# Long attention on one core: the shift products, the weighted sums and the banks for maxima rearranged

## Chip, cores and metric

One core of a Trainium2 chip runs the whole program. The metric is the device time of one execution in microseconds (us), the median of several executions; lower is better.

## What is computed

Four layers of cross-attention, each with a feed-forward part behind it, on 16 batches of 56 tokens. Layers 1 to 3 attend with 16 heads over 1500 keys of 64 numbers, and these three attentions are the "long attention" that the change touches. Cut to what matters, for one batch:

```
scores = jnp.einsum('bhsr,bhlr->bhsl', q_r, k_r)     # 16 heads x 56 tokens, 1500 keys
attn   = jax.nn.softmax(scores, axis=-1)
ctx_c  = jnp.einsum('bhsl,bld->bhsd', attn, kv_rope)
out    = ctx_lat.reshape(b, s, H * K) @ Wo.T
```

The softmax needs the maximum over the keys for each of the 16 x 56 = 896 rows (the shift, which is subtracted before the exponential) and the sum of the exponentials.

## The kernel before

`attend_long` runs one layer's long attention. Its queries stand as 64 numbers on partitions and 896 columns, cut in two halves e = 0 and 1 of 448 columns; the keys and queries are held twice, on partitions 0 to 63 and 64 to 127, so that products with 64 rows for e = 0 and e = 1 run side by side on the two row halves of TensorE's array. The 1500 keys are cut in 12 units of 125. A batch has three rounds of four units; there are 16 batches in a layer and three layers, so 48 batches and 144 rounds. In each layer batches 0 to 3 and 12 to 15 are written out, batches 4 to 11 run in a loop (`Fori`).

**Scores.** For a unit, `score` issues four steps (part 0 to 3) of two products each, e = 0 and 1: keys high x query high, keys low x query high, keys high x query low, and the shift. The last multiplies a tile of ones (`on`, 64 rows) with `sh`, whose row 64e holds the negated maxima and whose other rows are zero. All four add up in one PSUM bank for each e: unit u uses banks 2(u mod 2) and 2(u mod 2) + 1. The first part waits until ScalarE has taken the unit before the last out of them (`exp_done`), the last signals `st_ready`.

**Exponentials.** ScalarE's `exps` reads both banks of a unit (125 x 896) and writes one of four ring buffers `ex`.

**Weighted sums.** After the 16 steps of a round, PE issues `weigh` for the four units of that round in one burst: plain float32 products, values (125 rows x 64 columns) against `ex`, e = 0 to the lower and e = 1 to the upper 64 output columns. They go to bank 4.

**Maxima.** The next batches' maxima are computed ahead: 21 pieces in a batch (seven tiles of 128 query rows, three stretches of 500 keys), each one product with 64 rows (`top_scores`, alternating between the row halves) and one reduction on VectorE (`tops`), through banks 6 and 7; a piece waits until the piece before the last is reduced. `PLACES` says before which step of a round (0 to 16) each of its seven pieces goes. When all 21 are done VectorE reduces them to `nm` (128 x 7), PE turns `nm` through bank 5 with a float32 product (`turn`, after the burst of the second round), ScalarE copies the result (`high`), and SP moves it to `sh` with four DMAs (`shifts`).

**Row sums.** GpSimd and VectorE add the exponentials of a round up (`gather`, `pair`); after the first round of the next batch PE sums over partitions (`sums_by_quarters`, 32 output columns, bank 5) and ScalarE copies that out (`row_sums`). `numerators` copies bank 4 after the last burst of the batch, in ScalarE's order after the batch's exponentials.

**SP** runs one list for each batch b, behind a wait for all weighted sums of batch b - 1: loads of keys and queries for b + 2, of their low parts for b + 1, then the row sums, the shifts for b + 1, and the scales.

The lines are: 1174 score products, 1181 maxima products, 1196 turn, 1206 weighted sums, 1214 sums by quarters, 1271 and 1276 reductions of maxima, 1283 `pair`, 1341 exponentials, 1347 `numerators`, 1359 `high`, 1109 shift DMAs. Elsewhere in the program, and untouched: line 433 (products with 64 rows and 96 columns of weights), line 2145 (128 rows and 128 columns), line 133 (products that keep PE running).

Of the kernel before, what the change touches and what calls it, by code (L numbers as in the profile page):

```python
# [13 lines left out]
FP32 = mybir.dt.float32  # L14
# [998 lines left out]
def attend_long(nc, G, l, ctxT):  # L1013
# [10 lines left out]
    with Stage(nc, f"att{l}") as st:  # L1024
        kh, q, top, nm, nmh = (G[n] for n in ("kh", "qt", "top", "nm", "nmh"))
# [19 lines left out]
        WEIGHED, SUMMED = 4, 5  # L1045
# [16 lines left out]
        PLACES = (0, 0, 6, 8, 10, 14, 16)  # L1062
# [16 lines left out]
        with nc.Block() as block:  # L1079

            @block.sync
            def _(sp):
# [20 lines left out]
                def shifts(b):  # L1103
                    s = b % 2
                    sp.wait_ge(high_done, b + 1)
                    for e, at, tiles, a, z in ((0, 0, (0, 3), 0, 128), (0, 384, (3, 4), 0, 64),
                                               (1, 0, (3, 4), 64, 128), (1, 64, (4, NT), 0, 128)):
                        n = (tiles[1] - tiles[0]) * (z - a)
                        sp.dma_start(sh[64 * e:64 * e + 1, s, at:at + n].rearrange("o (t p) -> o t p", p=z - a).bitcast(FP32),
                                     nmh[tiles[0]:tiles[1], s, a:z].bitcast(FP32)).then_inc(m_in[s], 16)  # L1110
# [26 lines left out]
                sp.wait_ge(ones, 1)  # L1137
# [18 lines left out]
            def _(pe):  # L1156
                def products(s, u, e):

                    rows, keys = slice(64 * e, 64 * e + 64), slice(KP * u, KP * u + KP)
                    high = q[rows, s, HALF * e:HALF * e + HALF]  # L1160
                    return ((kh[rows, s, keys], high), (kl[rows, s % 2, keys], high),
                            (kh[rows, s, keys], ql[rows, s % 2, :]), (on[rows, :], sh[rows, s % 2, :]))

                def score(s, b, u, part, first):

                    if part == 0 and not (known(b, 1) and u < 2):
                        pe.wait_ge(exp_done, UNITS * b + u - 1)
                    if u == 0 and part == 1:
                        pe.wait_ge(kl_in[s % 2], of_two(s, b, 64))
                    if u == 0 and part == 3:  # L1170
                        pe.wait_ge(m_in[s % 2], of_two(s, b, 64))
                    for e in (first, 1 - first):
                        k, rhs = products(s, u, e)[part]
                        last = pe.matmul(PS[2 * (u % 2) + e][0:KP, 0:HALF], k, rhs, start=part == 0, stop=part == 3)  # L1174
                    if part == 3:
                        last.then_inc(st_ready, 1)

# [6 lines left out]
                def top_scores(s, b, n, half):  # L1184
# [3 lines left out]
                    if not (known(b, 1) and n < 2):  # L1188
                        pe.wait_ge(mx_done, PIECES * b + n - 1)
                    maxima(6 + (PIECES * s + n) % 2, s, n, half).then_inc(mx_ready, 1)  # L1190

                def turn(s, b):
                    pe.wait_ge(nm_ready, b + 1)
                    if not known(b, 2):
                        pe.wait_ge(sm_done, b - 1)
                    pe.matmul(PS[SUMMED][0:NT, 0:128], nm[:, s % 2, :], G["ident"][:, :],
# [12 lines left out]

                def sums_by_quarters(total):  # L1210
# [7 lines left out]
                def sums(totals):  # L1218

                    for n, total in enumerate(totals):  # L1220
                        for e in range(2):
                            last = pe.matmul(PS[SUMMED][64 * e:64 * e + 64, 0:HALF], one[:, :], total[:, e, :],
# [36 lines left out]
                pe.wait_ge(ones, 3)  # L1259
                emit(pe, batch)  # L1260
                pe.wait_ge(sm_done, B - 1)
# [6 lines left out]
            def _(dve):  # L1268
                def tops(s, b, n):
                    dve.wait_ge(mx_ready, PIECES * b + n + 1)  # L1270
                    dve.tensor_reduce(top[:, s % 2, n // NS, n % NS:n % NS + 1], PS[6 + (PIECES * s + n) % 2][:, 0:SB],  # L1271
                                      AX.X, ALU.max).then_inc(mx_done, 1)

                def shift(s, b):
                    dve.wait_ge(mx_done, PIECES * b + PIECES)
                    dve.tensor_reduce(nm[:, s % 2, :], top[:, s % 2], AX.X, ALU.max, negate=True).then_inc(nm_ready, 1)
# [20 lines left out]
                def batch(s, b, left):  # L1297
                    for i in range(UNITS // 4):
                        for place in range(17):
# [10 lines left out]
                for t in range(NT):  # L1310
# [3 lines left out]
                    dve.tensor_reduce(nm[:, 0, t:t + 1], scored, AX.XY, ALU.max, negate=True).then_inc(mx_done, NS)  # L1314
                dve.wait_ge(mx_done, PIECES)
                dve.engine_nop().then_inc(nm_ready, 1)
# [5 lines left out]
                dve.reciprocal(rsb[:, 1, :], PS[SUMMED][:, 0:HALF]).then_inc(last_inverted, 1)  # L1322
# [6 lines left out]
            def _(act):  # L1329
# [25 lines left out]
                def high(s, b):  # L1355
# [3 lines left out]
                    act.activation(nmh[:, s % 2, :], PS[SUMMED][0:NT, 0:128],  # L1359
                                   ACT.Copy).then_inc(high_done, 1)  # L1360

                def batch(s, b, left):
                    for i in range(UNITS // 4):
                        for u in range(4 * i, 4 * i + 4):
# [3 lines left out]
                        if i == 1 and left:  # L1368
                            high((s + 1) % 4, b + 1)
                    if left:  # L1370
                        numerators(s, b)
# [5 lines left out]
            def _(pool):  # L1377
                pool.wait_ge(G["q_out"][1], HALF_STORES * l)
# [25 lines left out]
                pool.wait_ge(ones, 3)  # L1404
# [1101 lines left out]
```

## Time and profile before

| | |
|---|---|
| median of 3 executions | 2348.38 us (2343.8 to 2348.43) |
| the profiled execution's own time | 2348.98 us |
| its span, first to last instruction | 2347.2 us |
| PE busy | 2203.3 us (94%) |
| PE weight loads busy | 1538.0 us (66%) |
| VectorE busy | 1476.7 us (63%) |
| GpSimd busy | 1093.4 us (47%) |
| ScalarE busy | 950.1 us (40%) |

Each stage of the program has its own limit, so the shares of the whole span say little about one of them; the stage is read by windows and by the timeline of one batch. PE's times in the trace are the start of a product and a modelled end: products that follow each other overlap there, so distances between starts tell the pace. A burst that the timeline merges ends with its last product, whose own duration has to be taken off to get that product's start.

### The profile page before, as it was taken

The page shows a single profiled execution, that of the slowest core. Times are in us where ns is not written, and L with a number is a line of the kernel's source. Part 1 is how long each engine was busy: PE and PEld are TensorE (multiplying, and loading weights), DVE is VectorE, ACT ScalarE, POOL GpSimd, SP SyncE. Part 2 cuts the span into 40 slices and gives each one's busy share as a digit, 9 for nine tenths or more (in the row PEclk, how much of TensorE's full clock was granted, in tenths as well). Part 3 has the DMA queues.
Part 4 walks back from the last instruction along what each step waited for, and adds up shares of the span by engine and source line. Part 5 has one row for each costly group of instructions (what it writes and reads, how often), then busy time and mean ns, then how long its engine had stood idle before and what let it go on. Part 6 is the DMA issues. An engine that isn't in the chain of part 4 may idle for free. (4 is left out here: it accounts for less than half of the span.)

```text
span 2347.2 us, 38608 instructions
## 1 busy us (share of the span) xinstructions
PE 2203.3 (94%) x13814; PEld 1538.0 (66%) x13814; DVE 1476.7 (63%) x2468; ACT 950.1 (40%) x1433; POOL 1093.4 (47%) x612
## 2 busy tenths in 40 slices
PE   6768999999999998999999999898999999998998
PEld 4447998665555557666555555897655555577997
DVE  2775444577777757787777775412777777744444
ACT  2442443434455442113544454112354455424443
POOL 0330332047777760563777777101177777722332
PEclk9878999999999999999999999898999999998999
DMA  4472732474555513226455451384845446303332
GB/s 83 131 249 84 224 116 81 114 174 99 136 116 116 121 30 126 60 81 149 99 124 128 103 135 30 123 336 181 237 94 129 110 108 136 74 5 111 116 116 82
DMA packets 124358, 285.60 MB, mean 122 GB/s; under 512 B 33371, under 2 KB 76207, under 8 KB 120476
## 3 DMA queue, kind: packets, MB, share of 16 engines
q1 hardware_dynamic: 123548, 281.96, 44.8%
q8 instruction: 82, 1.34, 0.3%
q0 software_dynamic: 672, 1.84, 0.2%
q14 instruction: 56, 0.46, 0.1%
HBM read 237.15 MB, written 46.41 MB: 121 GB/s over the span
## 5 line engine op out<-in xcount | busy, mean ns | idle before, releaser
L1271 DVE TENSOR_REDUCE keep_top<-banks 128x1 f32<-128x500 f32 x945 | 604.2, 675 | 241.9 <-PE banks L1181 236.3
L1341 ACT ACTIVATE att_ex<-banks 125x896 f32<-125x896 f32 x576 | 524.3, 919 | 236.3 <-PE banks L1174 216.8
L1206 PE MATMUL banks<-att_ex,att_v 125*64 125x448 f32 x2304 | 464.7, 545 | 0.0
L1394 POOL TENSOR_TENSOR att_acc<-att_acc,att_ex 125x896 f32<-125x896 f32 x186 | 391.8, 2106 | 74.0 <-ACT att_ex L1341 60.8
L1394 POOL TENSOR_TENSOR att_acc<-att_acc,att_two 125x896 f32<-125x896 f32 x141 | 297.2, 2108 | 161.4 <-DVE att_two L1283 161.4
L1181 PE MATMUL banks<-keep_kh,keep_qt 64*128 64x500 f32 x1230 | 369.8, 420 | 2.6 <-PEq L598 1.2
L1206 PEld LDWEIGHTS banks<-att_ex,att_v 125*64 125x64 f32 x2304 | 152.5, 136 | 247.1 <-issue 188.4
L1174 PE MATMUL banks<-att_sh,att_on 64*125 64x448 f32 x1152 | 296.7, 365 | 0.0
L1174 PE MATMUL banks<-att_ql,keep_kh 64*125 64x448 f32 x1152 | 296.1, 363 | 0.0
L1709 PE MATMUL banks<-moe_xs,moe_w 128*128 128x448 f32 x1272 | 285.6, 374 | 5.4 <-DVE moe_w L1805 3.8
L1283 DVE TENSOR_TENSOR att_two<-att_ex 125x896 f32<-125x896 f32 x144 | 243.1, 1688 | 59.6 <-ACT att_ex L1341 57.2
L1709 PEld LDWEIGHTS banks<-moe_xs,moe_w 128*128 128x128 f32 x1272 | 243.2, 192 | 31.1 <-DVE moe_w L1805 4.6
L1795 POOL TENSOR_TENSOR moe_sc<-moe_sg,moe_cb 128x448 f32<-128x448 f32 x106 | 122.5, 1156 | 292.5 <-ACT moe_sg L1767 263.1
L1174 PE MATMUL banks<-keep_qt,keep_kh 64*125 64x448 f32 x1152 | 246.7, 403 | 8.0 <-ACT att_ex L1341 2.7
L1181 PEld LDWEIGHTS banks<-keep_kh,keep_qt 64*128 64x128 f32 x1230 | 178.7, 187 | 86.7 <-issue 59.5
L1174 PE MATMUL banks<-keep_qt,att_kl 64*125 64x448 f32 x1152 | 217.4, 363 | 0.0
L1818 DVE TENSOR_TENSOR moe_hf<-banks,moe_sc 128x448 f32<-128x448 f32 x106 | 66.2, 625 | 201.4 <-POOL moe_sc L1795 201.4
L1174 PEld LDWEIGHTS banks<-att_sh,att_on 64*125 64x125 f32 x1152 | 177.3, 183 | 15.3 <-DMA att_sh<-keep_nmh 0.3
L1174 PEld LDWEIGHTS banks<-att_ql,keep_kh 64*125 64x125 f32 x1152 | 173.6, 183 | 6.4
L1174 PEld LDWEIGHTS banks<-keep_qt,keep_kh 64*125 64x125 f32 x1152 | 108.9, 182 | 74.5 <-ACT att_ex L1341 53.4
L1394 POOL TENSOR_TENSOR att_acc<-att_ex 125x896 f32<-125x896 f32 x48 | 101.1, 2107 | 103.2 <-ACT att_ex L1341 103.2
L789 POOL TENSOR_TENSOR q_tc<-q_tc,q_ts 96x896 f32<-96x896 f32 x32 | 67.6, 2111 | 113.0 <-DVE q_ts L777 113.0
(271 smaller groups left out, 2725.5 us busy)
## 6 DMA issues: line engine op xcount, KB each, us to landing
keep_kh<-kvt_hi SPq DMA_DIRECT2D x96, 375.0 KB, 5.2
att_kl<-kvt_lo SPq DMA_DIRECT2D x96, 375.0 KB, 7.3
q_rows<-mats_q SPq DMA_DIRECT2D x24, 896.0 KB, 4.9
keep_qt<-q_rows SPq DMA_DIRECT2D x96, 224.0 KB, 5.9
moe_raw<-L_experts_dram SPq DMA_DIRECT2D x53, 384.0 KB, 4.2
att_v<-kvn SPq DMA_DIRECT2D x24, 720.0 KB
sort_wu<-L_experts_dram SPq DMA_DIRECT2D x14, 1024.0 KB, 8.3
moe_cb<-comb_rows SPq DMA_DIRECT2D x62, 224.0 KB
```

The lines of the kernel that those rows point to most:

```text
L789: pool.tensor_tensor(tc[:, u % 4], tc[:, u % 4], ts[:, u % 2], ALU.add).then_inc(rot_done, 1)
L1174: last = pe.matmul(PS[2 * (u % 2) + e][0:KP, 0:HALF], k, rhs, start=part == 0, stop=part == 3)
L1181: return pe.matmul(PS[bank][:, 0:SB], q[rows, s, 128 * t:128 * t + 128], kh[rows, s, SB * c:SB * c + SB], start=True, stop=True)
L1206: last = pe.matmul(PS[WEIGHED][64 * e:64 * e + 64, 0:HALF], v[:, s // 2, u, s % 2, :], ex[:, u % RING, e, :], start=u == 0, stop=u == UNIT ...
L1271: dve.tensor_reduce(top[:, s % 2, n // NS, n % NS:n % NS + 1], PS[6 + (PIECES * s + n) % 2][:, 0:SB], AX.X, ALU.max).then_inc(mx_done, 1)
L1283: dve.tensor_tensor(two[:, i], ex[:, 2], ex[:, 3], ALU.add).then_inc(paired, 1)
L1341: act.activation(ex[:, u % RING], scored, ACT.Exp).then_inc(exp_done, 1)
L1394: pool.tensor_tensor(a, a if n else ex[:, 0], two[:, i] if k == 2 else ex[:, k], ALU.add).then_inc(gathered, 1)
L1709: last = pe.matmul(PS[2 * e + m][:, 0:HALF], w[:, s, pw, o:o + 128], xs[:, px, k, HALF * e:HALF * e + HALF], start=n == 0, stop=n == 3 * K ...
L1795: pool.tensor_tensor(sc[:, e, :], sg[:, e, :], cb[:, s, HALF * e:HALF * e + HALF], ALU.mult).then_inc(comb_done, 1)
L1818: dve.tensor_tensor(hf[:, e, :], PS[2 * e + 1][:, 0:HALF], sc[:, e, :], ALU.mult).then_inc(h_made, 1)
```

## The change

- **Shifts.** Steps 0 to 2 of a unit stay. The fourth, for one unit, goes; instead `shift_two` issues one step of four products for two units u (even) and u + 1, each on a strip of 32 rows (rows 0, 32, 64, 96 of `sh` and `on` start the strips), into the four banks of the two units. It closes unit u and opens unit u + 1, and stands between them. `free`, the wait for the bank, moves with it. A pair of units has seven steps instead of eight.
- **Weighted sums.** `weigh_two` issues the sums of two units, after step 6 (those of the two units before) and at the end of a round (those of its first two units). A round has two bursts of two units, lagging by two; the last two units of a batch are weighed in the first round of the next, and after the last batch on their own. `numerators` moves behind the second exponential of the next batch, and SP's list of a batch waits for that later burst.
- **Maxima.** Three banks 5, 6, 7 in turn; a piece waits for the piece three before. The row sums use bank 6 and the turn bank 7 in between, with waits for what was there (`mx_done`, `sm_done`, `high_done`). `PLACES` is new, for 15 places.
- **Turn.** `nm` becomes 64 x 128 (in the fast float32 format, zeroed at the start by GpSimd), written by two reductions of 64 partitions each; it is turned by one product with 64 rows and 64 columns against a small identity, at the start of the third round. `nmh` is 14 x 64, and the four DMAs each bring seven rows of 64 numbers. The first batch's maxima go the same way.

```diff
-        PLACES = (0, 0, 6, 8, 10, 14, 16)
+        PLACES = (1, 4, 6, 7, 9, 11, 13)
+        SHARED = 2 * NT + 2
...
+                    for row in range(0, 128, 32):
+                        a = NT * (row // 64)
+                        sp.dma_start(sh[row:row + 1, s, :].rearrange("o (g j) -> o g j", j=64).bitcast(FP32),
+                                     nmh[a:a + NT, s, :].bitcast(FP32)).then_inc(m_in[s], 16)
...
-                            (kh[rows, s, keys], ql[rows, s % 2, :]), (on[rows, :], sh[rows, s % 2, :]))
+                            (kh[rows, s, keys], ql[rows, s % 2, :]))
+
+                def free(b, u):
+                    if not (known(b, 1) and u < 2):
+                        pe.wait_ge(exp_done, UNITS * b + u - 1)
...
+                def shift_two(s, b, u):
+
+                    free(b, u + 1)
+                    if u == 0:
+                        pe.wait_ge(m_in[s % 2], of_two(s, b, 64))
+                    for odd in range(2):
+                        for e in range(2):
+                            rows = slice(64 * e + 32 * odd, 64 * e + 32 * odd + 32)
+                            last = pe.matmul(PS[2 * odd + e][0:KP, 0:HALF], on[rows, :], sh[rows, s % 2, :],
+                                             start=odd == 1, stop=odd == 0)
+                        if odd == 0:
+                            last.then_inc(st_ready, 1)
...
-                    maxima(6 + (PIECES * s + n) % 2, s, n, half).then_inc(mx_ready, 1)
+                    pe.wait_ge(mx_done, PIECES * b + n - 2)
+                    if n == SHARED and not known(b, 2):
+                        pe.wait_ge(sm_done, b - 1)
+                    if n == TURNED - MAXIMA:
+                        pe.wait_ge(high_done, b)
+                    maxima(MAXIMA + n % 3, s, n, half).then_inc(mx_ready, 1)
...
-                    pe.matmul(PS[SUMMED][0:NT, 0:128], nm[:, s % 2, :], G["ident"][:, :],
+                    pe.wait_ge(nm_ready, 2 * b + 2)
+                    pe.matmul(PS[TURNED][:, 0:64], nm[:, s % 2, :], eye[:, :],
...
+                def weigh_two(s, b, u):
+
+                    for v in (u - 2, u - 1):
+                        if v >= 0:
+                            weigh(s, b, v)
+                        elif not known(b, 1):
+                            weigh((s - 1) % 4, b - 1, UNITS + v)
...
                 def batch(s, b, left):
                     for i in range(UNITS // 4):
                         half = 0
-                        for place in range(17):
+                        if i == 2 and left:
+                            turn((s + 1) % 4, b + 1)
+                        for place in range(15):
                             for ahead, n in pieces(i, place, left):
                                 top_scores((s + ahead) % 4, b + ahead, n, half)
                                 half = 1 - half
-                            if place < 16:
-                                score(s, b, 4 * i + place // 4, place % 4, half)
-                        for u in range(4 * i, 4 * i + 4):
-                            weigh(s, b, u)
+                            u, step = 4 * i + place // 7 * 2, place % 7
+                            if place < 14:
+                                if step == 3:
+                                    shift_two(s, b, u)
+                                else:
+                                    score(s, b, u + step // 4, step % 4, half)
+                            if place == 6:
+                                weigh_two(s, b, u)
+                        weigh_two(s, b, 4 * i + 2)
                         if i == 0 and not known(b, 1):
                             pe.wait_ge(gathered, GATHERS * b)
-                            pe.wait_ge(high_done, b + 1)
+                            if left:
+                                pe.wait_ge(mx_done, PIECES * b + PIECES + SHARED - 2)
                             sums_by_quarters(acc[:, (s + 1) % 2])
-                        if i == 1 and left:
-                            turn((s + 1) % 4, b + 1)
...
+                    for side in range(2):
+                        dve.tensor_reduce(nm[:, s % 2, side:2 * NT:2], top[64 * side:64 * side + 64, s % 2],
+                                          AX.X, ALU.max, negate=True).then_inc(nm_ready, 1)
...
                         for u in range(4 * i, 4 * i + 4):
                             exps(b, u)
+                            if u == 1 and not known(b, 1):
+                                numerators((s - 1) % 4, b - 1)
```

## Rows read from the trace of the kernel before

**Rows 1.** The page: span, busy time of engines, tenths by slice, PE's clock.
```profile
span 2347.2 us, 38608 instructions
PE 2203.3 (94%) x13814; PEld 1538.0 (66%) x13814; DVE 1476.7 (63%) x2468; ACT 950.1 (40%) x1433; POOL 1093.4 (47%) x612
...
PE   6768999999999998999999999898999999998998
...
PEclk9878999999999999999999999898999999998999
```
**Rows 2.** Windows: length, busy (x) PE, PEld, DVE, ACT, POOL, clock, DMA share, GB/s.
```profile
1092.43:1116.54 24.11, 24.11 (x178) 13.99 (x176) 18.50 (x26) 12.21 (x15) 16.83 (x8) 1.00 0.42 94
1286.95:1311.39 24.44, 24.23 (x177) 14.30 (x175) 18.98 (x27) 12.08 (x16) 17.98 (x9) 1.00 0.52 118
```
**Rows 3.** Timeline, PE, one loop batch: start, length, engine, line, shapes, count.
```profile
1286.95 3.23 PE L1206 MATMUL banks<-att_ex,att_v 125*64 125x448 f32 x16
1290.11 0.39 PE L1196 MATMUL banks<-ident,keep_nm 128*7 128x128 f32 x2
1290.42 0.49 PE L1181 MATMUL banks<-keep_kh,keep_qt 64*128 64x500 f32 x2
1290.76 0.36 PE L1174 MATMUL banks<-keep_qt,keep_kh 64*125 64x448 f32 x2
...
1291.56 0.37 PE L1174 MATMUL banks<-keep_qt,keep_kh 64*125 64x448 f32 x2
...
1292.43 0.36 PE L1174 MATMUL banks<-att_sh,att_on 64*125 64x448 f32 x1
1292.82 0.47 PE L1174 MATMUL banks<-keep_qt,keep_kh 64*125 64x448 f32 x2
...
1294.79 0.39 PE L1181 MATMUL banks<-keep_kh,keep_qt 64*128 64x500 f32 x1
...
1295.11 3.23 PE L1206 MATMUL banks<-att_ex,att_v 125*64 125x448 f32 x16
1298.27 0.50 PE L1181 MATMUL banks<-keep_kh,keep_qt 64*128 64x500 f32 x2
...
1303.04 0.60 PE L1206 MATMUL banks<-att_ex,att_v 125*64 125x448 f32 x2
```
**Rows 4.** Timeline, PE, behind the first round's burst of that batch.
```profile
1306.19 0.58 PE L1214 MATMUL banks<-att_acc,att_one 125*32 125x224 f32 x8
1306.71 0.49 PE L1181 MATMUL banks<-keep_kh,keep_qt 64*128 64x500 f32 x2
1307.04 0.37 PE L1174 MATMUL banks<-keep_qt,keep_kh 64*125 64x448 f32 x2
```
**Rows 5.** Line 1206 from 1286.9 to 1290: ns min/median/max, first and last start.
```profile
L1206 PE MATMUL banks<-att_ex,att_v x16: 539/539/590, 1287.0 to 1289.6; 125*64 125x448 f32 x16
```
**Rows 6.** Line 1174, whole span, the same columns; who waited for it.
```profile
L1174 PE MATMUL banks<-keep_qt,keep_kh x1152: 356/365/733, 490.5 to 2071.2; 64*125 64x448 f32 x192
...
  ACT att_ex L1341: 216.8, 290
```
**Rows 7.** Another stage, timeline, PE: 64-row products, then 128-row ones.
```profile
915.49 0.36 PE L433 MATMUL banks<-weights_wkr,weights_wqr 64*96 64x64 f32 x1
915.78 1.33 PE L2145 MATMUL banks<-weights_wc,weights_wq 128*128 128x192 f32 x3
```
**Rows 8.** That place by windows, and line 2145 there.
```profile
914.60:916.80 2.20, 2.20 (x19) 2.08 (x18) 2.17 (x2) 0.91 (x2) 0.00 (x0) 0.50 0.00 0
...
L2145 PE MATMUL banks<-weights_wc,weights_wq x5: 527/528/687, 915.8 to 917.2; 128*128 128x192 f32 x5
```
**Rows 9.** Timeline, VectorE, end of a second round.
```profile
1286.59 1.26 DVE L1271 TENSOR_REDUCE keep_top<-banks 128x1 f32<-128x500 f32 x2 [0.31 <-PE banks L1181]
1287.89 0.17 DVE L1276 TENSOR_REDUCE keep_nm<-keep_top 128x7 f32<-128x21 f32 x1
1288.08 1.91 DVE L1283 TENSOR_TENSOR att_two<-att_ex 125x896 f32<-125x896 f32 x1
```
**Rows 10.** Timeline, ScalarE: copy of the sums, then two exponentials.
```profile
1273.95 0.55 ACT L1347 ACTIVATE att_cu<-banks 128x448 f32<-128x448 f32 x1 [2.39 <-PE banks L1206]
1275.34 1.94 ACT L1341 ACTIVATE att_ex<-banks 125x896 f32<-125x896 f32 x2 [0.84 <-PE banks L1174]
```
**Rows 11.** Timeline, SP's queue: shift DMAs, then the next batch's loads.
```profile
1266.22 2.72 SPq L1109 DMA_DIRECT2D att_sh<-keep_nmh  x4
...
1274.17 1.24 SPq L626 DMA_DIRECT2D keep_kh<-kvt_hi  x2
```

More of the change, by code:

```diff
@@ L1024, in attend_long @@
     with Stage(nc, f"att{l}") as st:
-        kh, q, top, nm, nmh = (G[n] for n in ("kh", "qt", "top", "nm", "nmh"))
+        kh, q, top, nm, nmh, eye = (G[n] for n in ("kh", "qt", "top", "nm", "nmh", "eye"))
         kl = st.sb("kl", [128, 2, L], F32R)
@@ L1136, in _ @@
                 load_values(0)
-                sp.wait_ge(ones, 1)
+                sp.wait_ge(ones, 3)
                 shifts(0)
@@ L1221, in sums @@
                         for e in range(2):
-                            last = pe.matmul(PS[SUMMED][64 * e:64 * e + 64, 0:HALF], one[:, :], total[:, e, :],
+                            last = pe.matmul(PS[LAST_SUMMED][64 * e:64 * e + 64, 0:HALF], one[:, :], total[:, e, :],
                                              start=n == 0, stop=n == len(totals) - 1)
@@ L1258, in _ @@
                         maxima(half, 1, n, half)
-                pe.wait_ge(ones, 3)
+                pe.wait_ge(ones, 5)
                 emit(pe, batch)
+                for u in range(UNITS - 2, UNITS):
+                    weigh(3, B - 1, u)
                 pe.wait_ge(sm_done, B - 1)
@@ L1298, in batch @@
                     for i in range(UNITS // 4):
-                        for place in range(17):
+                        for place in range(15):
                             for ahead, n in pieces(i, place, left):
@@ L1313, in _ @@
                     scored = PS.all[:, a:a + NS * 512].rearrange("p (c k) -> p c k", c=NS)[:, :, 0:SB]
-                    dve.tensor_reduce(nm[:, 0, t:t + 1], scored, AX.XY, ALU.max, negate=True).then_inc(mx_done, NS)
+                    dve.tensor_reduce(top[:, 0, t, 0:1], scored, AX.XY, ALU.max).then_inc(mx_done, NS)
                 dve.wait_ge(mx_done, PIECES)
-                dve.engine_nop().then_inc(nm_ready, 1)
+                dve.wait_ge(ones, 2)
+                for side in range(2):
+                    dve.tensor_reduce(nm[:, 0, side:2 * NT:2], top[64 * side:64 * side + 64, 0, :, 0:1],
+                                      AX.X, ALU.max, negate=True).then_inc(nm_ready, 1)
                 for n in range(NT):
@@ L1363, in batch @@
                     for i in range(UNITS // 4):
+                        if i == 2 and left:
+                            high((s + 1) % 4, b + 1)
                         for u in range(4 * i, 4 * i + 4):
                             exps(b, u)
+                            if u == 1 and not known(b, 1):
+                                numerators((s - 1) % 4, b - 1)
                         if i == 0 and not known(b, 1):
                             row_sums(b - 1)
[L1368 to L1371, printed above, removed]
                 high(0, 0)
@@ L1377, in _ @@
             def _(pool):
+                pool.memset(nm[:, :, :].bitcast(FP32), 0.0).then_inc(ones, 1)
+                pool.tensor_copy(eye[:, :], G["ident"][0:64, 0:64]).then_inc(ones, 1)
                 pool.wait_ge(G["q_out"][1], HALF_STORES * l)
@@ L1402, in place @@
                     pool.tensor_tensor(ctxT[:, :, b * S:b * S + S], c, r, ALU.mult).then_inc(placed, 1)
-                pool.wait_ge(ones, 3)
+                pool.wait_ge(ones, 5)
                 for b in range(B):
```

37 lines of the change are left out of this document (14 added, 23 removed).

## The prediction

> **What bounds the kernel now.** I read the page first: PE is busy for 94% of the span, at nearly full clock [rows 1]. Long attention is half of the program: 48 batches of some 24.3 us. The windows are cut from burst to burst of weighted sums, three rounds each. A batch that is written out takes 24.11 us with PE busy for all of it, one in the loop 24.44 us with 24.23 us busy, both at clock 1.00, while VectorE has 18.5 to 19.0 us of work, GpSimd 16.8 to 18.0 us and ScalarE 12.1 to 12.2 us [rows 2]. So PE sets the pace. Half the batches are loop batches, so I take 24.27 us as the mean. Busy does not mean streaming at full pace, so next comes the timeline of PE [rows 3, 4], read by distances between starts.
>
> A step of two products takes 0.20 us (four steps from 1290.76 to 1291.56, 0.203 each, which I use). Weighted sums: 16 instructions in two columns, eight distances between the burst's start at 1286.95 and the end of its work; the last one starts at 1286.95 + 3.23 - 0.54 = 1289.64 [rows 3, 5], so seven distances take 2.69 us: 0.375 each, and 0.05 more for the first, which is 0.590 long instead of 0.539 [rows 5]. Eight are 3.00 us.
>
> **What a change of shape costs.** The array is used in pieces of different shapes: 64 rows and all columns (scores, maxima), all rows and 64 columns (weighted sums), all rows and 32 columns (sums by quarters). From the last start of a burst to what follows is 1290.11 - 1289.64 = 0.47 us instead of 0.375: 0.095 late. The first product of the new shape then waits openly for its weights: the score products after the turn and the maxima come at +0.33 (1290.42 to 1290.76), where the 500 columns of a maxima product are worth 500/448 of 0.187, 0.21: 0.12 more. Into a burst it is 1295.11 - 1294.79 = 0.32 against 0.21 (0.10 late) and the 0.05 above. In and out of a burst together: 0.10 + 0.05 + 0.095 + 0.12 = 0.37 us; with 125 instead of 128 columns of weights I take 0.35.
>
> **A round without waiting.** 16 steps (3.25), the opening pair of maxima (0.33), five more pieces, three of them on the busier row half (3 x 0.21 = 0.62), into the burst (0.10): 4.30 us. Measured from the first maxima to the next burst: 1290.42 to 1295.11 = 4.69 and 1298.27 to 1303.04 = 4.77 [rows 3], and 1306.71 to 1311.39, the window's end, 4.68 [rows 2, 4]. So 0.41 us of a loop round is waiting. It lies where unit 2 opens: 1292.43 to 1292.82 is 0.39 instead of 0.20, and that product lasts 0.47 instead of 0.36, its weights come openly too. ScalarE's exponential of unit 0 is what it waits for: bank and exponential run in lockstep. A written-out batch is 0.33 us shorter, 0.1 a round, so on average 0.36 us a round is waiting.
> The whole round before is 4.30 + 3.16 (burst, 1295.11 to 1298.27) + 0.36 = 7.82 us, with 0.32 a batch for the turn (1290.11 to 1290.42) and 0.52 for the sums by quarters (1306.19 to 1306.71) [rows 3, 4]. Check: 3 x 7.82 + 0.84 = 24.3.
>
> **The change, part by part.**
> 1. *Waits for exponentials.* In the new order every wait has a burst in front of it. The exponential of an odd unit can begin at step 6 and is wanted at the next `shift_two`, behind a burst of 1.85 us and three steps; it needs 0.36 for the product to land and 0.92 (1.94 for two [rows 10] with a gap). That of an even unit is wanted at the next pair, behind three steps and a burst. Gain: 0.36 x 144 rounds = -52 us. ScalarE's `numerators` sits behind a burst that ends some 2.1 us after step 6, takes 0.55 [rows 10], and is over at 2.7, before the next shift's product at about 3.2: no cost; if that cover went, 0.5 us a batch.
> 2. *Two shift steps fewer a round.* Four became two: -2 x 0.203 = -0.41 us a round, -58 us, if four strips run side by side. No row shows four row strips. The nearest shows four column strips: eight products of 224 columns start within 0.52 - 0.095 us, that is, four in 0.2 [rows 4]. I take full overlap; the other end is two by two, +0.2 us a shift.
> 3. *Two bursts instead of one.* The products stay; one more in and out a round: +0.35 us, +50 us. It takes about what part 1 gives.
> 4. *The strips' own change of shape.* Scores use 64 rows, shifts 32, so each of the 288 shifts goes in and out. No row shows 64 against 32. The nearest change of rows alone is elsewhere: the last product of line 433 (64 rows) starts at 915.49, the first of line 2145 (128 rows, all columns as before) at 915.78, 0.29 later [rows 7]. This is at clock 0.50, 1.2 GHz [rows 8]. A float32 product of 64 columns costs 0.375 x 64/448 x 2 = 0.107 there. So it is 0.18 late, 0.09 at 2.4 GHz, the same 0.095 as above, and the first product is 0.687 long instead of 0.528 [rows 8], 0.16, or 0.08 at full clock, of open weight load. Rows alone thus cost what columns cost. One way: 0.095 + 0.08 to 0.12. Both ways: 0.35 to 0.43, I take 0.38. Ends: 0 (rows of 64 and 32 go together) and 0.43. 288 x 0.38 = +109 us.
> 5. *Turn.* One fast product of 64 columns in the shape of the scores replaces two slow ones with a shape of their own; 0.32 falls to about 0.1: -0.22 x 48 = -10 us. It now follows a burst of two units. VectorE ended the maxima at 1287.85 and their reduction at 1288.06, 1.1 us after that burst's start [rows 9]. With two reductions (0.17 each) and a piece issued one step before the burst, I expect 1.2 to 1.5 us, and the turn is due at 1.65. No cost, with little to spare.
> 6. *Three banks.* Before, pieces waited in no visible place; they still don't. The new wait of the sums by quarters is for a piece issued before that burst of 1.65 us, done in 1.1 to 1.4. No cost. Behind both waits stands all of PE's queue, so being late would be paid in full.
> 7. *SP.* Its list for a batch starts 3.7 us later. Loads went out at 1274.17 [rows 11] and the first of them are wanted at the third round, some 16 us later: nothing. The shift DMAs take 2.72 to issue [rows 11] and are wanted one round later; four again. GpSimd's zeroing and VectorE's extra reduction at a layer's start: +0.4 us a layer, +1.
>
> The sum a round: 12 steps 2.44; four stretches with one piece on the busier half, 4 x 0.21 = 0.83; two bursts of 1.50 + 0.35, 3.70; two shifts of 0.20 + 0.38, 1.16: 8.13 us against 7.82, +0.31. In the parts it is -0.36 - 0.41 + 0.35 + 0.76 = +0.34. I take +0.33 x 144 = 48, -10 for the turn, +1: **+39 us**. The profiled execution took 2348.98 us, 1.8 us more than its span and 0.6 above the median. Forecast 2348.98 + 39 = **2388 us**, with part 4's price between 0.30 and 0.43 and 10 us for the small terms between 2365 and 2412.
>
> The Trainium skill, in "TensorEngine Tiling (Array Packing)", section Tiling Modes, Key Properties, says "Changing tiling mode (not just tile) drains the TensorE", and lists 64-row and 32-row tiling as two modes. The 0.29 us of [rows 7] agree for 64 against 128 rows; no row shows 64 against 32. By this rule the change loses, as the forecast does. The skill's "TensorE: Matmul & The Clock Gate", Part 3, gives 3.07 times for four row strips instead of four. As an estimate from that page a shift would take 1.30 steps, and the sum would be 288 x 0.06 = 17 us more; [rows 4] speak for full overlap of column strips only.
>
> **The rivals.**
> - *Strips of 32 rows mix freely with 64* (part 4 costs nothing). For it: both cut the array in rows only, and weights of one row half load under products of the other all the time. Against it: [rows 7]. Time: 2388 - 109 = 2279 us (2262 to 2300). This is the one on the other side: the sum turns at a price of 0.38 - 39/288 = 0.245 us a shift; below that the change is faster.
> - *The array drains, but the weights are loaded by then* (0.19 a shift): 2388 - 0.19 x 288 = 2333 us.
> - *New waits take the place of the old.* Turn and sums by quarters come late because VectorE's `pair` (1.91 here beside GpSimd [rows 9]) gets ahead of the last pieces: 0.3 us each, 0.6 x 48 = 29: 2417 us.
> - *Four strips run two by two*: 288 x 0.2 = 58: 2446 us.
>
> **How the numbers follow.** Forecast 0.69, free mixing 0.16, drain alone 0.08, new waits 0.04, two by two 0.03. 0.2%, or 4.7 us, is about what a measurement of this kernel can tell from no change. Faster: 0.16 + 0.08 = 0.24. Same: 0.04, taken from the forecast's chance for a price near 0.245 us a shift. Slower: 0.65 + 0.04 + 0.03 = 0.72. The forecast's own range is 2365 to 2412. Since the other sign has a quarter, the range goes down into free mixing and up to the new waits: 2285 to 2422.
>
> **What would show it.** Shift products with 32 rows some 0.29 us after the step before, and the step after them 0.38 later with a first product of 0.46: part 4 right; distances of 0.20: free mixing. No ScalarE wait before line 1174 (216.8 us of ScalarE's own waiting for scores [rows 6] would grow): part 1. Bursts of eight instructions and 1.85 us from in to out: part 3. Batches of about 25.1 us: the sum. The forecast is wrong above all if the small change of rows is cheaper than the large one.

## The result and the profile after

The changed kernel takes **2403.52 us** in the median (2401.56 to 2410.25), against 2346.09 us for the kernel before (2339.82 to 2348.43): 1.0255 times as long over all executions, 95% interval 1.0234 to 1.0276 (the two medians alone give 1.0245). The forecast was 2388 us, slower, in a range up to 2422; so the direction and the range hold, and the loss is 57 us by the medians where 39 were forecast. The forecast added its 39 us to 2348.98 us, an execution 3 us above the median, so the time itself is off by less than the loss.

The page of the changed kernel, its span, engine shares, clock and some of the costliest groups (columns as in [rows 1] and in the section of groups):

```profile
span 2400.9 us, 38704 instructions
PE 2254.9 (94%) x13766; PEld 1462.9 (61%) x13766; DVE 1403.5 (58%) x2519; ACT 948.7 (40%) x1433; POOL 1090.9 (45%) x618
...
PEclk9878999999999998999999999888999999998999
...
L1383 ACT ACTIVATE att_ex<-banks 125x896 f32<-125x896 f32 x576 | 525.6, 919 | 503.8 <-PE banks L1190 479.9
...
L1190 PE MATMUL banks<-att_sh,att_on 32*125 32x448 f32 x1152 | 136.4, 464 | 1.8 <-DMA att_sh<-keep_nmh 1.8
```

PE executes 48 instructions fewer and is busy 52 us longer: the same share of a longer span, so the loss is in PE's own pace, not in idle time. ScalarE now waits 479.9 us for scores where it waited 216.8 [rows 6], but most of that rise is waiting that stood in front of its other copies before: its idle time as a whole went from 1397.1 to 1452.2 us (span less busy time), no more than the span grew. What shows that PE no longer waits for it is PE's timeline. A window over one loop batch, then PE's timeline of half a round (columns as in [rows 2] and [rows 3]; lines 1177 are the score products, 1198 the maxima, 1190 the shifts, 1224 the weighted sums, 1214 the turn):

```profile
619.88:645.26 25.38, 25.38 (x176) 12.59 (x174) 17.20 (x28) 12.10 (x16) 17.90 (x9) 1.00 0.44 101
```
```profile
632.57 0.36 PE L1177 MATMUL banks<-att_ql,keep_kh 64*125 64x448 f32 x2
632.86 1.72 PE L1224 MATMUL banks<-att_ex,att_v 125*64 125x448 f32 x8
634.52 0.50 PE L1198 MATMUL banks<-keep_kh,keep_qt 64*128 64x500 f32 x1
634.52 0.46 PE L1177 MATMUL banks<-keep_qt,keep_kh 64*125 64x448 f32 x1
...
634.86 0.36 PE L1177 MATMUL banks<-keep_qt,keep_kh 64*125 64x448 f32 x1
...
635.25 0.38 PE L1177 MATMUL banks<-att_ql,keep_kh 64*125 64x448 f32 x2
635.56 0.47 PE L1190 MATMUL banks<-att_sh,att_on 32*125 32x448 f32 x4
635.96 0.48 PE L1198 MATMUL banks<-keep_kh,keep_qt 64*128 64x500 f32 x1
635.96 0.47 PE L1177 MATMUL banks<-keep_qt,keep_kh 64*125 64x448 f32 x1
636.27 0.36 PE L1177 MATMUL banks<-keep_qt,att_kl 64*125 64x448 f32 x1
...
636.69 0.37 PE L1177 MATMUL banks<-att_ql,keep_kh 64*125 64x448 f32 x2
636.99 0.60 PE L1224 MATMUL banks<-att_ex,att_v 125*64 125x448 f32 x2
```

All is there to be read. The four shift products run together (four in 0.47 us, the length of one). They start 0.31 us after the start of the last score step (635.25 to 635.56), where a step is 0.20; what follows comes 0.40 later, and the step after that another 0.31 instead of 0.20, with a first product of 0.47 instead of 0.36. The burst of two units stands between 632.86 and 634.52, 1.66 us for 1.50 of products, with the same open wait for weights behind it. No distance is left that would be a wait for ScalarE, as 0.39 us at unit 2 was [rows 3]. A half round is 4.13 us (632.86 to 636.99), and six of them with 0.1 for the turn and 0.5 for the sums by quarters are the 25.38 us of the batch, against 24.11 and 24.44 [rows 2].

There is one more loss, of another kind, in the same trace. At the end of the first pass of the third layer's loop PE stands idle twice with no semaphore to wait for, and runs at a lower clock behind it:

```profile
1924.91 1.72 PE L1224 MATMUL banks<-att_ex,att_v 125*64 125x448 f32 x8
...
1928.32 0.47 PE L1177 MATMUL banks<-keep_qt,keep_kh 64*125 64x448 f32 x2 [1.68 <-issue]
1931.11 0.78 PE L1198 MATMUL banks<-keep_kh,keep_qt 64*128 64x500 f32 x1 [2.33 <-issue]
```
```profile
1924.91:1935.07 10.16, 6.16 (x29) 3.11 (x27) 3.58 (x7) 1.92 (x3) 2.71 (x2) 0.74 0.10 28
```

This half round takes 10.16 us instead of 4.13, and the clock granted over it is 0.74 instead of 1.00: behind the second pause, from 1931.1 to 1935.07, it is 0.50, the lower level of 1.2 GHz, and the products there are longer (0.78 us for a maxima product instead of 0.38). The next burst is still 0.8 us late (2.41 us instead of 1.66 to what follows), so it is 7 us in all, once.

The profile gives a hint at what these pauses are. It lists a DMA queue that brings instructions, here its line for the kernel before, then for the changed one (transfers, MB, share):

```profile
q8 instruction: 82, 1.34, 0.3%
```
```profile
q8 instruction: 91, 1.49, 0.3%
```

A loop is two passes of four batches. In the kernel before this queue brings nothing during the second pass in the third layer (1890 to 1990 us), nor does it in the changed kernel in the first and second layer (700 to 800 and 1305 to 1405 us). In the changed kernel's third layer it goes on through the second pass (six transfers from 1930 to 2030 us), with one more inside PE's second pause. So the pauses stand where instructions are brought once more. That PE waited for them is likely, but argued, not shown.

### The profile page after: what moved, and what is told of

It is laid out like the page before. It is cut to its first block and busy times, and to the rows that moved or that the text cites. A ratio compares the mean times of both kernels' runs of the same rounds, so it can differ in the third digit from the quotient of the medians.

```text
span 2400.9 us, 38704 instructions
## 1 busy us (share of the span) xinstructions
PE 2254.9 (94%) x13766; PEld 1462.9 (61%) x13766; DVE 1403.5 (58%) x2519; ACT 948.7 (40%) x1433; POOL 1090.9 (45%) x618
## 5 line engine op out<-in xcount | busy, mean ns | idle before, releaser
L1383 ACT ACTIVATE att_ex<-banks 125x896 f32<-125x896 f32 x576 | 525.6, 919 | 503.8 <-PE banks L1190 479.9
L1224 PE MATMUL banks<-att_ex,att_v 125*64 125x448 f32 x2304 | 496.6, 552 | 0.0
L1198 PE MATMUL banks<-keep_kh,keep_qt 64*128 64x500 f32 x1230 | 445.0, 430 | 5.5 <-POOL keep_eye L1421 3.2
L1177 PE MATMUL banks<-keep_qt,keep_kh 64*125 64x448 f32 x1152 | 363.5, 429 | 1.7 <-issue 1.7
L1177 PE MATMUL banks<-keep_qt,att_kl 64*125 64x448 f32 x1152 | 334.0, 364 | 0.0
L1177 PE MATMUL banks<-att_ql,keep_kh 64*125 64x448 f32 x1152 | 247.6, 362 | 0.0
L1322 DVE TENSOR_TENSOR att_two<-att_ex 125x896 f32<-125x896 f32 x144 | 161.4, 1121 | 90.5 <-ACT att_ex L1383 89.0
L1177 PEld LDWEIGHTS banks<-keep_qt,att_kl 64*125 64x125 f32 x1152 | 202.3, 184 | 1.6
L1177 PEld LDWEIGHTS banks<-keep_qt,keep_kh 64*125 64x125 f32 x1152 | 152.6, 182 | 67.9 <-ACT att_ex L1383 43.8
L1177 PEld LDWEIGHTS banks<-att_ql,keep_kh 64*125 64x125 f32 x1152 | 139.9, 183 | 6.9
L1190 PE MATMUL banks<-att_sh,att_on 32*125 32x448 f32 x1152 | 136.4, 464 | 1.8 <-DMA att_sh<-keep_nmh 1.8
```

Source lines behind the costliest of these rows:

```text
L1190: last = pe.matmul(PS[2 * odd + e][0:KP, 0:HALF], on[rows, :], sh[rows, s % 2, :], start=odd == 1, stop=odd == 0)
L1198: return pe.matmul(PS[bank][:, 0:SB], q[rows, s, 128 * t:128 * t + 128], kh[rows, s, SB * c:SB * c + SB], start=True, stop=True)
L1224: last = pe.matmul(PS[WEIGHED][64 * e:64 * e + 64, 0:HALF], v[:, s // 2, u, s % 2, :], ex[:, u % RING, e, :], start=u == 0, stop=u == UNIT ...
L1322: dve.tensor_tensor(two[:, i], ex[:, 2], ex[:, 3], ALU.add).then_inc(paired, 1)
L1383: act.activation(ex[:, u % RING], scored, ACT.Exp).then_inc(exp_done, 1)
```

## The experiments

Each is compared with the kernel before on its own chip; the kernel before had medians of 2342.0 to 2344.7 us there.

### The shape alone, in the kernel before

```diff
-                            (kh[rows, s, keys], ql[rows, s % 2, :]), (on[rows, :], sh[rows, s % 2, :]))
+                            (kh[rows, s, keys], ql[rows, s % 2, :]), (on[64 * e:64 * e + 32, :], sh[64 * e:64 * e + 32, s % 2, :]))
```

> The kernel before with one edit: each shift product uses 32 rows of ones and shifts instead of 64. Count, columns, order and waits stay. Theory (each visit to another row count costs the change of shape both ways, 0.386 us as the trace after shows it): 576 visits x 0.386 = 222 us, of which up to some 40 fall into time that PE waited for ScalarE anyway: 2525 to 2570 us. Rival (the loss after came from four strips writing four banks at once, or from the new order of opening and closing banks; rows of 32 and 64 mix freely): no change, 2346 us.

Measured: 2555.07 us, 1.0896 times the kernel before (1.0878 to 1.0914). PE's timeline in the second half of a round:

```profile
648.06 0.46 PE L1174 MATMUL banks<-att_sh,att_on 32*125 32x448 f32 x2
648.46 0.49 PE L1181 MATMUL banks<-keep_kh,keep_qt 64*128 64x500 f32 x1
...
649.19 0.38 PE L1174 MATMUL banks<-att_ql,keep_kh 64*125 64x448 f32 x2
649.50 0.47 PE L1174 MATMUL banks<-att_sh,att_on 32*125 32x448 f32 x2
649.89 0.47 PE L1174 MATMUL banks<-keep_qt,keep_kh 64*125 64x448 f32 x2
650.21 0.37 PE L1174 MATMUL banks<-keep_qt,att_kl 64*125 64x448 f32 x2
```

Same products, same count, same order: 211 us for 576 visits to the other row count, 0.366 us a visit. The 0.40 us from shift to next (648.06 to 648.46) and the longer first products are those of the changed kernel. In the middle of a round the distances are 0.31, 0.39 and 0.32 us (649.19, 649.50, 649.89, 650.21) where three plain steps take 0.61, so a visit costs 0.41 there. The 0.366 are net: where unit 2 opens the distance is that same 0.40, so the wait for ScalarE that the kernel before had at this place is hidden under the change of shape. The rivals are out: 32 rows don't mix with 64, and no four strips are needed for the loss.

### The strips alone undone

```diff
-                            rows = slice(64 * e + 32 * odd, 64 * e + 32 * odd + 32)
+                            rows = slice(64 * e, 64 * e + 64)
...
-                pool.memset(on[:, :].bitcast(FP32), 1.0).then_inc(ones, 1)
+                pool.memset(on[:, :].bitcast(FP32), 0.5).then_inc(ones, 1)
```

> The changed kernel with the strips alone undone: the four shift products of a pair stay in their place, but use 64 rows (ones replaced by halves, since two rows hold the shift), so they are two steps in the shape of the scores. Theory (change of shape): each of 288 shifts loses 0.386 us and gains one step of 0.203: 2403.5 - 53 = 2351 us, the shares of the other edits then being +50 (bursts), -50 (waits), -10 (turn) and some 15 left over. Rival (the price is the second burst or new waits, not the strips): 2400 us or more, since a step is added.

Measured: 2348.47 us, 1.0018 times the kernel before (1.0004 to 1.0033). The strips cost 2403.5 - 2348.5 = 55 us, 0.19 us for each of 288 shifts; they account for nearly the whole loss. A loop batch of this kernel:

```profile
623.51:647.76 24.25, 24.25 (x177) 14.55 (x175) 17.77 (x28) 12.12 (x16) 17.85 (x10) 1.00 0.46 105
```

25.38 - 24.25 = 1.13 us in a batch, six shifts of 0.19. With halves instead of ones the two rows that hold the shift add up to it, so the result is the same. This trace too has the idle PE behind the first pass of the third layer's loop:

```profile
1877.15 0.46 PE L1177 MATMUL banks<-keep_qt,keep_kh 64*125 64x448 f32 x2 [1.35 <-issue]
1879.96 0.78 PE L1198 MATMUL banks<-keep_kh,keep_qt 64*128 64x500 f32 x1 [2.34 <-issue]
```

### The two bursts alone undone

```diff
-                            if place == 6:
-                                weigh_two(s, b, u)
-                        weigh_two(s, b, 4 * i + 2)
+                        for u in range(4 * i, 4 * i + 4):
+                            weigh(s, b, u)
...
-                for u in range(UNITS - 2, UNITS):
-                    weigh(3, B - 1, u)
```

> The changed kernel with the bursts alone undone: one burst of the round's four units at the end of the round, strips, banks and turn as changed. Theory: a burst's way in and out, 0.35 us x 144 = 50 us, goes, and the wait for the exponentials between the pairs of a round comes back, 0.2 to 0.5 us a round, 29 to 72 us: 2383 to 2425 us, about 2400. Rival (the lagging bursts are free or the waits they removed were worth more): above 2425; rival (the waits were not removed by the bursts): 2353 us.

Measured: 2391.17 us, 1.0198 times the kernel before (1.0181 to 1.0215): 12 us faster than the changed kernel. Taking the second burst out gives more than the waits that it had removed take back. Some 7 of the 12 us are the pauses behind the loop's first pass, which this version's trace doesn't have; the other 5 are what a second burst costs above the waits that it removes.

### Both undone

The two edits above together.

> Both undone: 64-row shift products, one burst of four units a round; what is left of the change is the three banks, the places of the pieces and the new turn. Theory: the kernel before minus the turn's 10 us, with the same waits for exponentials or a little less: 2330 to 2340 us, faster than both kernels. Rival (banks and places cost something): 2346 us or more.

Measured: 2359.58 us, 1.0065 times the kernel before (1.0048 to 1.0082). **A miss**: with bursts and strips as before, it should have been faster than the kernel before, and is 15 us slower. PE's timeline shows two waits in a round where the kernel before had one [rows 3] (first start of the round at 639.33):

```profile
641.32 0.36 PE L1177 MATMUL banks<-att_ql,keep_kh 64*125 64x448 f32 x1
641.81 0.47 PE L1177 MATMUL banks<-keep_qt,keep_kh 64*125 64x448 f32 x2
...
642.54 0.35 PE L1177 MATMUL banks<-att_ql,keep_kh 64*125 64x448 f32 x1
642.84 0.67 PE L1190 MATMUL banks<-att_sh,att_on 64*125 64x448 f32 x4
643.35 0.36 PE L1177 MATMUL banks<-keep_qt,keep_kh 64*125 64x448 f32 x1
```

The first is the old one (641.32 to 641.81, 0.49 before unit 2). The second stands before the shifts (0.30, and 0.51 for two steps behind it): `shift_two` waits for the bank of the pair's second unit before it issues the first unit's shift, which doesn't need that bank. That shift is what lets ScalarE begin.

### The wait for the second bank moved

On top of the two edits above:

```diff
-                    free(b, u + 1)
                     if u == 0:
                         pe.wait_ge(m_in[s % 2], of_two(s, b, 64))
                     for odd in range(2):
+                        if odd == 1:
+                            free(b, u + 1)
```

> The kernel with both undone (64-row shifts, one burst), with one line moved: the wait for the bank of the pair's second unit stands behind the first unit's shift products instead of ahead of them. Theory (in the changed order the first unit's shift, and so its exponential, waits for the bank of the second unit, which it does not need; two bursts a round had hidden this): the second wait of a round, 0.1 us late and 0.1 us of open weight load, goes where it stood in front of an exponential, so 0.1 to 0.2 us x 144 come back: 2330 to 2345 us. Rival (the 15 us that this kernel was slower than the kernel before come from banks, places or the new turn): 2360 us still.

Measured: 2335.01 us, 0.9966 times the kernel before (0.9954 to 0.9979), and faster than both kernels. One line is worth 1% here, 23 us by the two ratios (1.0065 and 0.9966). In the changed kernel itself the same line costs nothing, since a burst stands before it: only 1.1 us of idle time before the shifts, over the whole span, are put down to line 1383. What is left of the change in this version is the banks, the places, the turn and one line's place: 7 us of gain, with 10 forecast for the turn.

### Strips right behind the burst

The strip step opens both units of a pair instead of standing between them, so that a pair passes three changes of shape, not four. The score products no longer open a bank, and the third step closes each unit (that part of the edit isn't shown).

```diff
-                                if step == 3:
+                                if step == 0:
                                     shift_two(s, b, u)
                                 else:
-                                    score(s, b, u + step // 4, step % 4, half)
+                                    score(s, b, u + (step - 1) // 3, (step - 1) % 3, half)
...
-                            last = pe.matmul(PS[2 * odd + e][0:KP, 0:HALF], on[rows, :], sh[rows, s % 2, :],
-                                             start=odd == 1, stop=odd == 0)
-                        if odd == 0:
-                            last.then_inc(st_ready, 1)
+                            pe.matmul(PS[2 * odd + e][0:KP, 0:HALF], on[rows, :], sh[rows, s % 2, :],
+                                      start=True, stop=False)
```

> The changed kernel with the strip step moved: the four 32-row products open both units of a pair right behind the burst that stands in front of it, instead of standing between the two units. Theory (what costs is the number of changes of shape): a pair passes scores, sums, strips, scores, three changes instead of four; one change, 0.095 us late and 0.10 us of open weight load, goes 288 times: 2403.5 - 56 = 2348 us, if ScalarE has emptied both banks by then (1.4 us after the last score against 1.85 us of burst). Rival (what costs is the strip step itself, wherever it stands): 2403 us; rival (the earlier wait for the banks bites): 0.3 us a pair, 2430 us.

Measured: 2406.11 us, 1.026 times the kernel before (1.0242 to 1.0278). **A miss**, by the figure of the rival, but not by its mechanism:

```profile
616.96 1.72 PE L1219 MATMUL banks<-att_ex,att_v 125*64 125x448 f32 x8
...
620.88 1.72 PE L1219 MATMUL banks<-att_ex,att_v 125*64 125x448 f32 x8
622.53 0.49 PE L1193 MATMUL banks<-keep_kh,keep_qt 64*128 64x500 f32 x1
622.96 0.47 PE L1187 MATMUL banks<-att_sh,att_on 32*125 32x448 f32 x4
623.36 0.47 PE L1175 MATMUL banks<-keep_qt,keep_kh 64*125 64x448 f32 x2
...
625.22 1.72 PE L1219 MATMUL banks<-att_ex,att_v 125*64 125x448 f32 x8
```

A single maxima piece (622.53), left where `PLACES` had it, stands between burst and strips, in the shape of the scores: the fourth change of shape was back, with a product that has the array to itself. Such a half round takes 4.34 us (620.88 to 625.22), one without the piece 3.92 (616.96 to 620.88), against 4.13 in the changed kernel: what one gains the other loses. The turn did the same once a batch.

### The same, with nothing between

On top of the edit above, the piece and the turn move behind the strips:

```diff
-        PLACES = (1, 4, 6, 7, 9, 11, 13)
+        PLACES = (1, 4, 6, 8, 9, 11, 13)
...
-                        if i == 2 and left:
-                            turn((s + 1) % 4, b + 1)
                         for place in range(15):
+                            if i == 2 and left and place == 1:
+                                turn((s + 1) % 4, b + 1)
```

> The strips behind the burst once more, now with nothing of another shape between them: the piece that stood ahead of the second pair's first step and the turn, both in the shape of the scores, move behind the strip step. In the trace of the run before, half rounds with such a piece took 4.35 us and one without it 3.92, and the one with the turn 4.15. Theory (the number of changes of shape): 2406 us - 48 x 3 x 0.43 (pieces) - 48 x 0.2 (turn) = 2335 us, 10 us faster than the kernel before. Rival (the strips' wait for both banks costs right behind the burst): 2350 us or more, with PE waiting for ScalarE ahead of the 32-row products.

Measured: 2360.78 us, 1.0078 times the kernel before (1.0063 to 1.0093): 45 of the 71 us that were expected against the version before. The batch shows the theory's price:

```profile
624.64:648.86 24.22, 24.22 (x176) 13.11 (x174) 17.11 (x28) 11.53 (x16) 17.86 (x9) 1.00 0.44 97
```

24.22 us, below the 24.44 of a loop batch before. But 21 times a batch opens late, and the trace says on what; first PE, then SP's own queue (start, length, line, what is issued):

```profile
668.12 0.47 PE L1187 MATMUL banks<-att_sh,att_on 32*125 32x448 f32 x4 [1.18 <-DMA att_sh<-keep_nmh]
```
```profile
651.75 0.93 SPq L1101 DMA_DIRECT2D att_v<-kvn  x2
652.73 0.56 SPq L1116 DMA_DIRECT2D rs_rows<-att_sm  x1
663.51 0.35 SPq L1119 DMA_DIRECT2D att_rin<-rs_rows  x1
663.91 3.05 SPq L1110 DMA_DIRECT2D att_sh<-keep_nmh  x4
```

SP issues the first DMA of the row sums (3.5 KB) at 652.73, right behind the batch's loads, and waits until 663.51 for it to land, 10.8 us. In the kernel before the list sends the same DMA some 3 us after its loads, and the two issues are 4.2 or 8.0 us apart:

```profile
1258.21 0.56 SPq L1115 DMA_DIRECT2D rs_rows<-att_sm  x1
1262.39 0.33 SPq L1118 DMA_DIRECT2D att_rin<-rs_rows  x1
...
1282.86 0.57 SPq L1115 DMA_DIRECT2D rs_rows<-att_sm  x1
1290.86 0.35 SPq L1118 DMA_DIRECT2D att_rin<-rs_rows  x1
```

Short and long alternate from batch to batch: 3.3 to 5.0 and 7.4 to 8.7 us before, 6.9 to 7.8 and 9.2 to 11.1 here, so the later list costs this DMA some 3 us. The shifts were ready at 659.85 and go out at 663.91. PE's idle time before line 1187 that is put down to the shift DMA is 16.7 us.

### Shift DMAs first on SP

On top of the edit above:

```diff
+                def sums_back(b):
+
                     sp.wait_ge(sum_out, 16 * b + 16)
...
                     if b < B - 1:
                         shifts(b + 1)
                     if b:
+                        sums_back(b - 1)
                         scales(b - 1)
```

> The kernel with the strips behind the burst and nothing between, with one edit on SP: the shift DMAs for the next batch are issued ahead of the second DMA of the row sums instead of behind it. In the trace of that kernel SP sits from 652.73 to 663.51 us for the first row-sum DMA to land behind the batch's loads, while the shifts are ready at 659.85, and PE idles 16.7 us in all for the landing of the shifts, which the strips want as a batch's first step. Theory (SP's queue, shifted by the lagging burst, is what kept that kernel from its 2335 us): 2361 - 17 = 2344 us, level with the kernel before, and no idle time of PE put down to the shift DMA. Rival (the rest is the banks' wait or small terms): 2358 us or more.

Measured: 2347.08 us, 1.0006 times the kernel before (0.9994 to 1.0017). The idle time of PE before the shifts of this kernel that is put down to the shift DMA (us, times):

```profile
  DMA att_sh<-keep_nmh: 4.1, 3
```

So 16.7 us became 4.1, and 0.7% of the time, 14 us in the medians and 17 by the ratios, are gone. Of the 26 us between the 2335 expected of the version before and its 2361, some 10 stay unexplained. Strips are thus worth nothing in the best place tried: level with the kernel before, level with the version with 64 rows and two bursts (1.0018, with 7 us of pauses in its loop that this one doesn't have), and 0.4% (some 9 us) behind the version with 64 rows and one burst.

## Why the prediction was right, and where it was short

- **Part 4, the strips' change of shape: right, mechanism and size.** It rested on one row of another stage, 64 against 128 rows at half the clock [rows 7, 8]; that the smaller change of rows costs as much as the larger was assumed, and a quarter of the chances stood against it. Undone alone, each of 288 shifts turned out to cost 0.19 us more than the two plain steps in its place; as one step of 0.20 is saved, the change of shape costs 0.39 for both ways. The 576 visits of the first experiment give 0.366 net of a hidden wait, and 0.41 by distances; 0.38 was forecast. With the step saved in part 2, -58 + 109 = 51 us was forecast for the strips, and 55 measured by undoing them alone.
- **Part 2: right.** Four row strips ran together, four products in the time of one. The distance from the shift to what follows is 0.40 us with four strips (635.56 to 635.96), and 0.39 to 0.40 with two in the first experiment (649.50 to 649.89, 648.06 to 648.46). The rival "two by two" is out. The estimate worked out from the Trainium skill's 3.07 times ("TensorE: Matmul & The Clock Gate", Part 3), 0.06 us more a shift, isn't borne out by these distances.
- **The rule of the Trainium skill** ("TensorEngine Tiling (Array Packing)", Tiling Modes), that a change of tiling mode drains TensorE: the runs agree for 32 and 64 rows, with 0.366 us net for both ways in the first experiment.
- **Part 1: right** in that no wait for ScalarE was left in PE's timeline above, and only 1.1 us of PE's and its weight loads' idle time before the shifts is put down to it. That ScalarE's wait for scores would grow came true as well (216.8 to 479.9 us), but proves little, as said above.
- **Parts 1 and 3 together: mis-sized.** Forecast: -52 for the waits, +50 for the second burst, -2. Measured between the version with 64-row shifts and two bursts (ratio 1.0018) and the one with a single burst and the late wait (0.9966): 0.52% or 12 us for bursts instead of waits. About 7 of these are the pauses behind the loop's first pass, which only the former's trace has; some 5 are left, 0.04 us a round, with an uncertainty of about 4 from the two intervals. A batch of the former is 24.25 us, so a round without turn and sums is (24.25 - 0.62)/3 = 7.88 us, where 7.46 + 0.35 = 7.81 were forecast. In the timeline above it is the burst's way out: a step next to a piece comes 0.34 us after it (634.52 to 634.86) where 0.21 of product and 0.10 of weights make 0.31.
- **Part 5: right.** The turn takes 0.1 instead of 0.32 us: the half round with it is 4.22 us (bursts at 628.64 and 632.86), the others 4.13.
- **Part 6 and the new waits: right** that they cost nothing; VectorE ended the two reductions at 629.81 us and the turn stood at 630.29, behind its burst.
- **Part 7: right in the sum, wrong in its reason.** "Loads 3.7 us later: nothing" looked at who wants the loads, and not at what stands behind them in SP's list. In the changed kernel too the row sums' DMA goes out right behind them and the next issue is 10.5 us later (648.85 to 659.39), where the kernel before had 4.2 or 8.0, and the shifts wait with it. There the shifts are wanted at the fourth step of a batch and PE idles for them 1.8 us in all, so nothing was lost; with the strips as the first step it was 16.7.
- **Not foreseen:** the 7 us behind the loop's first pass. The miss of 18 us in the loss is then 4 (strips), 7 (bursts against waits, 5 where -2 was forecast) and 7 (loop), each known only to a few us, since the runs scatter by as much. That the parts come out even with the whole is in part luck.

What the pauses behind the loop are stays open. They occur in the traces of the changed kernel and of the one with the strips undone, at the same place of the same layer, not in the other two layers and not in the other versions. No semaphore releases PE there. The same two traces, and no others, have 91 transfers of instructions instead of 82. Why the instructions are brought once more in that layer of these two versions isn't known, and neither is whether it happens in every execution, as each trace shows one. No experiment was made on it.

## What to carry to other kernels

Products that use fewer rows of the array saved a step here and lost it again, because their neighbours had another shape: count the changes of shape along PE's order first, at 0.2 us each way here, and only then the products. A neighbour can undo the order by one stray product, so read the timeline for it after each edit. A wait belongs directly before the first instruction that needs it, and a list that moves on a DMA queue moves all that waits behind it.

## What the runs showed of the hardware that was not expected

- The change between 32 and 64 rows costs about as much as the one into the weighted sums and out (64 rows and all columns to all rows and 64 columns, 0.35 to 0.37 us by the prediction's rows): 0.39 us undone alone, 0.366 net in the first experiment, for products of 0.19 us.
- VectorE's addition of two ring buffers (`pair`, 125 x 896) took 1.96 us in the median before and 1.09 after, with the same instruction. By tile, line 1283 of the kernel before, then line 1322 of the changed one (ns min/median/max):

```profile
L1283 DVE TENSOR_TENSOR att_two<-att_ex x144: 1091/1960/2442, 496.0 to 2073.1; 125x896 f32<-125x896 f32 x144
```
```profile
L1322 DVE TENSOR_TENSOR att_two<-att_ex x144: 1091/1093/1759, 494.5 to 2132.2; 125x896 f32<-125x896 f32 x144
```

  In the kernel before it came while GpSimd's addition was running, as at 1263.37, where it took 1.98 us and ended 0.95 after GpSimd's (1264.40), nearly the 1.09 that it takes alone; in the changed order it comes while GpSimd waits for it. So the two additions hardly overlap. VectorE's busy time fell by 73 us (1476.7 to 1403.5), with 51 instructions more. VectorE wasn't the bound, so nothing was gained.
- A DMA of 3.5 KB that SP issues right behind ten loads took 6.9 to 11.1 us from its issue to the next one that waited for it, and 3.3 to 8.7 us when SP issued it some 3 us after the loads, both alternating from batch to batch. Without loads in front, in the last two batches of a layer, it took 1.6 to 2.1 us.
